# A two-layer graph network on one core: loads moved behind the x1 stores, zero multiplications added there, and a ring of twenty gathered rows

## The reference

```
x1  = layernorm(x + relu(segment_sum(norm * (x @ W)[src], dst) + b))      # self loops included
out = layernorm(x1 + layer1(x1, src, dst, edge_attr_20, edge_weight, edge_attr_3))
```

## Time and profile before

| | us |
|---|---|
| median of three runs | 1079.65 |
| lowest, highest | 1079.17, 1084.14 |
| the profiled execution | 1074.51 |
| its span, first to last instruction | 1072.70 |

### The profile page before, as it was taken

How to read it: one execution, slowest core, us unless ns; L and a number is a source line. 1 busy time by engine, 2 the same in 40 slices (tenths; PEclk the granted TensorE clock), 3 DMA queues, 4 the chain that set the end, 5 groups by cost and what they waited for, 6 DMA issues and landing times.

```text
span 1072.7 us, 17283 instructions
## 1 busy us (share of the span) xinstructions
PE 920.3 (86%) x4812; PEld 743.0 (69%) x4812; DVE 846.7 (79%) x2396; ACT 707.3 (66%) x1642; POOL 652.9 (61%) x945
## 2 busy tenths in 40 slices
PE   7889888999973999999999389999999999915553
PEld 7767777777753888887888268888887888714443
DVE  7688888886824788788889578888888888719997
ACT  4669877777761566666666446666666666638886
POOL 4028888888851566666666345776677676426665
PEclk9989999998995999999999789999999999955555
DMA  9989999999998499999998767999999999688995
GB/s 350 418 274 250 242 237 240 239 240 242 236 224 279 165 341 324 327 315 313 323 323 311 273 187 178 216 206 218 226 217 211 216 228 189 94 220 337 389 400 233
DMA packets 121443, 280.39 MB, mean 261 GB/s; under 512 B 13746, under 2 KB 38342, under 8 KB 121350
## 3 DMA queue, kind: packets, MB, share of 16 engines
q1 hardware_dynamic: 73590, 186.25, 47.9%
q0 software_dynamic: 35280, 82.63, 40.0%
q10 hardware_dynamic: 12480, 10.42, 3.0%
HBM read 132.38 MB, written 146.87 MB: 260 GB/s over the span
## 4 chain that ended last, share of the span: by engine, by line
PE 43%; DVE 11%; DMA 8%; issue 4%; ACT 2%; POOL 1%; SPq 1%; ACTq 0%; DVEq 0%; POOLq 0%
PE bank L1309 8%; PE bank L1357 7%; PE bank L1340 6%; PE bank L1371 5%; DVE stat L1167 4%; PE bank L1313 4%; PE bank L1369 3%; DMA edge_mem<-x 3%; PE bank L1334 3%; PE bank L1300 2%; PE bank L1367 2%; DMA G_mem<-x 2%; PE bank L1346 2%; DVE node_mem L1158 1%; DVE stat L1043 1%
## 5 line engine op out<-in xcount | busy, mean ns | idle before, releaser
L548 POOL DMA_INDIRECT sum<-R_mem,sidx_all x79 | 129.1, 1634 | 85.0 <-DMA sum<-zeros 48.7
L609 POOL DMA_INDIRECT sum<-R_mem,l_sidx x79 | 135.6, 1717 | 45.9 <-issue 21.9
L595 POOL DMA_INDIRECT G_mem<-x_d,dst_i x79 | 77.2, 977 | 90.9 <-PE bank L1344 64.3
L1309 PE MATMUL bank<-G_hi 128*128 128x512 f32 x316 | 131.4, 416 | 0.0
L1309 PE MATMUL bank<-G_lo,G_hi 128*128 128x512 f32 x316 | 124.9, 395 | 0.0
L1225 PE MATMUL bank<-G_hi,M_mem 128*128 128x512 f32 x200 | 86.3, 432 | 7.0 <-ACT R_mem L681 6.4
L1313 PE MATMUL bank<-G_hi,G_lo 128*128 128x512 f32 x316 | 85.3, 392 | 0.0
L1114 DVE SCALAR_TENSOR_TENSOR edge_mem<-edge_mem,Y,bank 128x128 f32<-128x128 f32 x237 | 71.2, 385 | 15.0 <-ACT edge_mem L806 15.0
L1340 PE MATMUL bank<-edge_mem,Winv 128*128 128x512 f32 x158 | 81.8, 600 | 0.1
L1225 PE MATMUL bank<-G_lo,M_mem 128*128 128x512 f32 x200 | 80.5, 402 | 0.0
L1387 PE MATMUL bank<-ident,node_mem 128*128 128x128 f32 x80 | 27.5, 447 | 61.5 <-DVE node_mem L1158 61.5
(11 more groups left out here) (230 smaller groups left out, 2831.5 us busy)
## 6 DMA issues: line engine op xcount, KB each, us to landing
node_mem<-sum SPq DMA_DIRECT2D x41, 512.0 KB, 5.9
filt_d<-node_mem SPq DMA_DIRECT2D x40, 512.0 KB, 4.9
node_mem<-filt_d SPq DMA_DIRECT2D x79, 256.0 KB, 4.9
sum<-zeros SPq DMA_DIRECT2D x33, 512.0 KB, 14.2
G_mem<-x SPq DMA_DIRECT2D x20, 512.0 KB, 6.9
x_d<-node_mem SPq DMA_DIRECT2D x20, 512.0 KB, 3.5
edge_mem<-x SPq DMA_DIRECT2D x19, 512.0 KB, 6.1
x_d<-R_mem SPq DMA_DIRECT2D x19, 512.0 KB, 3.9
```

What stands on the lines that cost most here:

```text
L548: pool.indirect_dma_start(sum0, bass.IndirectOffsetOnAxis(ap=sidx[:, t:t + 1], axis=0), R[t % 8][:, :], None, compute_op=ALU.add).then_inc ...
L595: pool.indirect_dma_start(G3[t % 8][:, :], None, x1_d, bass.IndirectOffsetOnAxis(ap=dst_i[:, t:t + 1], axis=0)) \
L609: pool.indirect_dma_start(sum1, bass.IndirectOffsetOnAxis(ap=l1_sidx[0:n, t:t + 1], axis=0), R3[t % 8][0:n, :], None, compute_op=ALU.add). ...
L1309: pe.matmul(bank[4 + a][:, :], zT_hi[a][:, c * P:(c + 1) * P], w[c][:, :], start=(c == 0 and w is W0h), stop=False)
```

## The change

Four things.

1. `NG` goes from 12 to 20: the ring `G0` has eight more places, in `keep`, which is free in this stage. GpSimd gathers 12 tiles as before, then waits for `w_pre` at 1 and gathers eight more, ahead of its wait for the zeros. In the loop a group's gathers are now those of five groups ahead, so that the last of them follow group 14 and not 16.
2. In the node stage SP's four `trow` loads and four `filt` loads are issued after the last store of x1, filter rows first, and the wait for the transposes between them goes. The `sum1` stores of the last four pairs come after these loads. VectorE normalises the last two tiles and ScalarE the 77 before them.
3. TensorE gets `keep_clock`: fp32 matmuls of 128x512 zeros into bank 7, whose result nobody reads. Three follow a wait for all first-stage scatters, ahead of the node stage; three follow a wait for the last two pairs of `x1_d` stores, ahead of the second edge stage; two come ahead of its step 5 and one ahead of its step 6.
4. The helper `held` and its four semaphores go; its four uses become plain waits for the same values.

```diff
-        NG = 12
-        G0 = G + [b[:, 2 * D:3 * D] for b in node_mem]
+        NG = 20
+        G0 = G + [b[:, 2 * D:3 * D] for b in node_mem] + views(4 * D, 8, D, keep)
...
-                if j == T2 + 1:
-                    for g in range(4):
-                        trow_in(g)
-                    sp_.wait_ge(n_tr, TR)
-                    for t in range(4):
-                        filt_in(t)
                 if j >= 6:
                     i = j - 6
-                    sp_.wait_ge(n_x1, min(2 * i + 2, TR - 1))
-                    if i == T2 - 1:
-                        sp_.wait_ge(n_last, 1)
+                    sp_.wait_ge(n_x1, min(2 * i + 2, TR - 2))
+                    if i >= T2 - 2:
+                        sp_.wait_ge(n_last, i - T2 + 3)
                     sp_.dma_start(layer_pair(x1_d, i, 0, D), in_pair(res2[i % 8], i, 0, D)).then_inc(n_st[i % 8], 16)
-                    for k in ((i,) if i < T2 - 2 else (i - 1, i) if i == T2 - 1 else ()):
-                        sp_.dma_start(layer_pair(sum1, k, C, D), in_pair(res2[k % 8], k, C, D)).then_inc(rows_st[k % 8], 16)
+                    if i < T2 - 4:
+                        sum1_out(i)
+
+            def sum1_out(k):
+                sp_.dma_start(layer_pair(sum1, k, C, D), in_pair(res2[k % 8], k, C, D)).then_inc(rows_st[k % 8], 16)
 
             for j in range(T2 + 6):
                 nodes0(j)
+            for t in range(4):
+                filt_in(t)
+            for g in range(4):
+                trow_in(g)
+            for k in range(T2 - 4, T2):
+                sum1_out(k)
...
             for t in range(NG):
+                if t == 12:
+                    pool.wait_ge(w_pre, 1)
                 gather0(t)
...
-                    if t8 < TR - 1:
+                    if t8 < TR - 2:
                         act.activation(r, r, ACT.Identity, bias=tiny[b][:, 6, k:k + 1], scale=tiny[b][:, 5, k:k + 1]).then_inc(n_x1, 1)
...
-            dve.wait_ge(n_root, 2 * K_RSTD)
-            r = res[(TR - 1) % 16]
-            dve.tensor_scalar(r, r, w[:, 5, 0:1], w[:, 6, 0:1], ALU.mult, ALU.add).then_inc(n_last, 1)
+            for t in (TR - 2, TR - 1):
+                g, k, r = t // 2, t % 2, res[t % 16]
+                dve.wait_ge(n_root, K_RSTD * (g - T2 + 3))
+                dve.tensor_scalar(r, r, tiny[g % 4][:, 5, k:k + 1], tiny[g % 4][:, 6, k:k + 1], ALU.mult, ALU.add).then_inc(n_last, 1)
...
+            def keep_clock(b, n):
+                for _ in range(n):
+                    pe.matmul(bank[b][:, :], zeros[:, 0:P], zeros[:, 0:512], start=True, stop=True)
...
             ins.then_inc(s_pairs, 1)
+            pe.wait_ge(e_scat, 16 * TR)
+            keep_clock(7, 3)
...
+            for u in (6, 7):
+                pe.wait_ge(n_st[u], 16 * (T2 // 8))
+            keep_clock(7, 3)
 
             def edges1(s, u):
+                if s in (5, 6):
+                    keep_clock(7, 7 - s)
```

More of the change, by code:

```diff
@@ L377, in build @@
         rows_st = [sem(f"rows_st{i}") for i in range(8)]
[L379 to L387, removed]
         NZ = 8
@@ L565, in nodes0 @@
                     st.mark(pool.tensor_scalar(w[:, 7, :], mean, -1.0, None, ALU.mult))
-                    held(pool, n_rs, 2 * (g + 1))
+                    pool.wait_ge(n_rs, 2 * (g + 1))
                     st.mark(pool.tensor_tensor(w[:, 3, :], w[:, 2, :], w[:, 2, :], ALU.mult))
@@ L569, in nodes0 @@
                     st.mark(pool.tensor_tensor(w[:, 4, :], w[:, 3, :], w[:, 0, :], ALU.mult))
-                    held(pool, n_rstd, st.reached())
+                    pool.wait_ge(n_rstd, st.reached())
                     st.mark(pool.tensor_scalar(w[:, 3, :], w[:, 4, :], -0.5, 1.5, ALU.mult, ALU.add))
@@ L780, in nodes0 @@
                     t9 = s - 11
-                    if t9 < TR - 1:
+                    if t9 < TR - 2:
                         act.wait_ge(n_x1, t9 + 1)
                     else:
-                        act.wait_ge(n_last, 1)
+                        act.wait_ge(n_last, t9 - TR + 3)
                     act.copy(xs1[t9 // 2][:, t9 % 2 * C:(t9 % 2 + 1) * C], res[t9 % 16][:, 0:C]).then_inc(n_keep, 1)
@@ L828, in edges1 @@
                     t, a = s - 2, (u - 2) % 8
-                    held(act, f_gather[a], 16 * (turn(t, a, 8) + 1))
+                    act.wait_ge(f_gather[a], 16 * (turn(t, a, 8) + 1))
                     wait(act, f_tr, t - 3)
```

## The result

The changed kernel takes 1086.85 us (median of 21 runs, 1082.97 to 1093.75) where the kernel before takes 1079.17 (21 runs beside it). The ratio of the two is 1.0071, 95% interval [1.0059, 1.0084]: 7.7 us slower. The forecast was 6.5 us more, at 1086.1.

The account below looks back on a forecast made before the run. Middle stages bound by TensorE, first edge stage by GpSimd, last by VectorE at the low clock. 1.8 - 1.6 + 5.0 + 1.3 = +6.5 on the 1079.65 us median gives 1086.1; range 1075 to 1092.

Parts of the forecast that it names:

- The ring: First edge stage: eight gathers moved to about 52 us make it 1.8 us longer, bounds -1.6 and +5.
- The delay of the first scatter: First edge stage: gather traffic makes the zeros end later, moving the first scatter from 69.71 to 74.7 us, +5.0.
- The wait of the fourth scatter (-1.6): First group of the first edge stage: the fourth scatter's 1.65 us wait for ScalarE goes, -1.6 us.
- The late groups (-1.6): End of the first edge stage: three groups without gathers fall to 12.64 us, with the group before summing to -1.6.
- Zeros ahead of the node stage: Node stage start: three multiplications delay the first transpose 0.9 us, clock rises at 342.5; -1.6 us, bounds -2.8 and +0.9.
- The transition: Into the second edge stage: ScalarE's first step waits for the last sum1 stores until 621 us, +5.0, bounds 0 and +8.
- Rival (c): Transition: queues take strict turns, last sum1 store lands at 623.5 to 624, +8 instead of +5, total 1089.1; chance 0.16.
- The 2.4 us of gain for the gather: Transition: the last x1 lands earlier, so the first gather can start near 610.2 instead of 612.58 us.
- Zeros around the second edge stage: Second edge stage: first three buy nothing, those ahead of steps 5 and 6 cost; sum +1.3, bounds -1.5 and +2.9.
- (a): Transition: stores land quickly, last sum1 near 617.5 instead of 621 us, +3.0 in all, total 1082.7; chance 0.18.
- (b): Second edge stage: joint loads' gain comes through, ScalarE starts at 616, clock stays high; -6.2, total 1073.5; chance 0.10.
- (d): First edge stage: GpSimd's issue paces to the end, eight gathers take 10 us off; -1.9, total 1077.8; chance 0.14.

Follow-up runs that it names:

- gather_first: Kernel before with the new order, zeros ahead of the node stage, ScalarE's sum1 wait later, and SyncE's loads held until the first gather lands: 1075.93 us, ratio 0.9956.

## Why the prediction came out right, and where its steps were wrong

**1. The ring, +1.8.** Measured +0.8 in late executions and +7.8 in early ones. The steps were worked out on the profile of before, an early one, and there two of them failed. The delay of the first scatter was right: 74.94 with the ring alone and 74.65 in the changed kernel, against 74.7. The wait of the fourth scatter (-1.6) did not go but grew by 1.0: I had said myself that the calculation slips too, because an rbf load stands behind the zeros, and then took the wait off in full, holding that the calculation slips less than the scatter. It slipped more, since TensorE waited 4.44 us for that load and then worked at the low clock. The late groups (-1.6) did not fall to 12.64 us: the first scatters of the last five groups span 51.8 us in the kernel before (271.41 to 323.23), 53.3 with the ring alone and 54.0 in the changed kernel, where 5.6 to 7.4 us of waiting stand ahead of each and the earlier trace rows had 5.13. So the term of -1.6 was +1.5 to +2.2; why the landings take longer without gathers between them stays open. One late group of before, with a wait that was the shortest of its kind, was no fair price for the others. That the term came near the truth as measured beside the changed kernel (0.8) is luck and no merit of the working: it is the late execution that hides the zeros.

**The base.** This was in view. The profiled execution stood 5.1 us below the median, and I carried the terms over from the one to the other as if the distance were noise. The profile was an early execution, the three runs (1079.17 to 1084.14) lie where the late ones do, and the stall of 7 us in the prologue that separates them changes what is on the critical path in the first edge stage. Had the runs been early ones, the parts would give 7.8 + 7.4 - 1.4 + 0.8 = 14.6 us, more than twice the forecast. The unaltered changed kernel was not measured in an early series; the version with the later wait is the nearest to it.

**2. Zeros ahead of the node stage, -1.6.** Measured -1.4. The mechanism is shown: the zeros begin with the last landing, the transposes behind them start 0.8 us after the old time, and the clock rises at 341.7 (worked out from its mean of 0.58 from 340 to 342) instead of 346.7.

**3. The transition, +5.0.** The mechanism is the right one, shown by the order alone and by the exchange of stores and loads, and supported by the version that waits later. The size was short: +7.4 [+5.6, +9.3] us, ScalarE at 623.3 where 621 stood. The term that was mis-sized is the rate. The bytes were right: 5.8 MB expected, 5.76 MB moved from 606.5 to 623.3 us (and 0.2 just before), of them 2.10 by the gathers (1.9 expected), which moved 1.47 MB in the 7 us from 614 to 621, 210 GB/s where 195 were allowed for. But the mean rate was 343 GB/s and not 391; at 391 the 5.76 MB would have ended at 621.2, the time that the prediction worked out. The largest part is lost from 611 to 614, where the trow loads are under way: 212 GB/s with the engines busy 0.92 of the time. The trace of before had this price in it, in the stretch in which the same loads land:

```profile
595.00:599.00 4.00, 3.71 (x17) 2.75 (x15) 3.93 (x10) 2.78 (x9) 2.17 (x9) 1.00 0.85 179
```

What makes these loads slow, no run varied. Rival (c) hit the landing (623.5 to 624), but its condition can't be told apart from the forecast's here: from 614 to 621 both queues moved about the same (1.47 and 1.38 MB), which is what turns would give, and equally the 195 GB/s of the earlier trace rows and the rest. The Trainium skill, "DMA: Bandwidth & Descriptors", section "Queues, rings and completion order", has the engines take turns between queues by the packet; these shares agree with it. The 2.4 us of gain for the gather were right as to its issue (3.0 us earlier with the order alone) and worth nothing, since beside the loads it lands 6.9 us after its issue instead of 3.5.

**4. Zeros around the second edge stage, +1.3.** Measured +0.8 by the ratios and +0.1 by the medians, within its uncertainty nothing. As forecast the three that wait for the x1 stores are wasted. A stretch table of the changed kernel:

```profile
620.00:622.00 2.00, 1.63 (x3) 0.21 (x1) 0.00 (x0) 0.00 (x0) 1.57 (x2) 0.66 0.75 227
622.00:624.00 2.00, 0.00 (x0) 0.00 (x0) 0.00 (x0) 0.00 (x0) 1.52 (x2) 1.00 1.07 409
624.00:626.00 2.00, 0.00 (x0) 0.00 (x0) 0.00 (x0) 0.00 (x0) 1.39 (x3) 0.69 1.03 409
```

They raise the clock just when they end (616.33 to 621.6); TensorE has nothing to do until 633.28, and from 626 the clock stands at 0.50. The multiplications ahead of step 5 then run at the low clock, 3.62 us for two. How much each of the term's three parts was off, no run tells.

**The sum** for late executions by measured parts: 0.8 - 1.4 + 7.4 + 0.8 = 7.6, the changed kernel 7.7 to 8.6 (by the medians 6.3 to 8.1). The order's 7.4 and the node clock's -1.4 in it come from the early series. That the order costs the same in late ones is borne out by the profiles: from VectorE's last normalisation to ScalarE's first step it takes 18.8 us with the order alone (early) and 19.0 to 19.9 in the five late profiles with this order, against 11.1 to 11.5 in five with the old one, early and late. The changed kernel without the ring (+9.2 [+5.8, +12.5] where the parts give 6.8) and the gain of the exchange agree with it. Against the forecast of 6.5 the ring came out 1.0 lower and the zeros around the second edge stage 0.5, the transition 2.4 higher and the node clock 0.2, so the total was 1.1 short. The total was near because the errors are small beside it and in part cancel, and because the runs were late ones.

The rivals: (a) fell, the stores did not land quickly; (b) fell: in `gather_first` its gain came only with the loads held back behind the gather and ScalarE's wait moved; (c) hit the landing time, by a condition that the trace can't separate from the forecast's; (d) fell, the bare groups did not get quicker.

## What to carry to other kernels

When a profiled execution lies off the median by as much as the effects that are asked about, look for the place where it differs before any term is carried from one to the other; and compare variants only within a series that shares its runs of the old kernel. When stores or loads change their order on a queue, ask of each transfer which engine waits for it and what bytes now land ahead of it or beside it, and price each kind of transfer by its own stretch: here the last sum stores stood behind 1.7 MB that nobody needed yet, the gather ran beside them, and a part of these bytes moved at half the rate of the others. An engine's wait belongs right ahead of the instruction that needs it, so that nothing else queues behind it. The zero multiplications paid where work followed them at once (ahead of the node stage) and not where it came 12 us later.

## What was not expected of the hardware

- One program has two courses of its first 60 us, 7 us apart, and mostly a whole series of runs shows one of them: 1070.1 to 1075.0 us in all 17 runs of before in one series, 1077.4 to 1085.0 in all 18 of another on the same chip. (The profile of before, 1074.51 us, is an early execution beside runs of 1075.46 us and more.) In the late profiles TensorE, VectorE and ScalarE idle together for some microseconds at a time between 14 and 24 us: from 5 to 27 us they are busy 13.02, 14.15 and 6.79 us in the changed kernel's profile, 18.82, 20.00 and 12.66 in that of before, while DMA moves 390 GB/s in both. What it is stays open; no run varied it.
- Full DMA engines don't always move the same: while the trow loads are under way the DMA engines are 0.85 to 0.92 busy and move 179 to 212 GB/s, where 391 to 417 are usual in the earlier trace rows.
- The time of a small gather depends on what else is queued: 3.4 to 3.5 us from issue to use with idle queues, 6.9 beside 1.7 MB of loads. The last store of 192 KB took 11.7 us behind the same loads in the changed kernel, where the median of all `sum1` stores is 4.4.
